# Score tiles begun by a ScalarE copy of the negated row maxima instead of a fourth product, with attention's steps in another order, in a one-core decoder layer

## The chip, the cores and the metric

One core of a Trainium2 chip runs the whole layer in one launch. The metric is device time in microseconds, the median of the runs of the program.

## What is computed

The reference is a decoder layer on `x` of 4 x 1024 x 256 (float32): attention with 16 heads of width 64, a convolution that shifts a memory, and a top-1 routed feed-forward layer, each followed by a layer norm. The change is in attention alone:

```python
q = einsum('bnd,hde->bhne', query, Wq) * scale
k = einsum('bmd,hde->bhme', query, Wk)
v = einsum('bmd,hde->bhme', query, Wv)
logits = einsum('bhne,bhme->bhnm', q, k)
attn = softmax(logits, axis=-1)
out = einsum('bhnm,bhme->bnhe', attn, v)
```

## The kernel before

**Units and halves.** Attention runs over 64 units. A unit is one pair of heads and 512 of the 1024 query tokens (`BANK`); its keys come in 8 tiles of 128. A unit is worked in two halves of four key tiles, so there are 128 halves, h = 0 to 127. All engines walk the same list of steps, `all_steps()`, each picking the steps that have work for it. Each half has its order written out by hand, in one of the four lines of `STEPS` (h modulo 4); a round below is four lines, two units.

**The steps** (functions of `build_attention`):
- `bite`: a projection of q, k or v, TensorE (lines 1123 and 1116) into a spare bank. q and k are kept as a high and a low float32r part. ScalarE copies the high part out (`bite_hi`, L1259), VectorE then makes the low part from the bank (`bite_lo`, L1315) and so frees the bank. For v ScalarE alone reads the bank.
- `pass`: 128 query rows against 512 keys with the high parts only, one matmul for each of the two heads (L1139), into two spare banks. It serves the row maxima of the unit ahead: VectorE reads each bank with a reduction by maximum (L1328), which frees it. After a unit's eighth pass VectorE negates and transposes the maxima (L1333, L1338), and SyncE moves them into `shift_rows` with four small DMAs (`move_shift`, L913).
- `score`: one tile of 128 keys x 512 queries x 2 heads into one of two score tiles `score_ps` (L1161). It takes four products, each a pair of matmuls with 64 rows, one for each head: k_hi q_hi, k_hi q_lo, k_lo q_hi, and ones times `shift_rows`, which adds the negated maximum of each query. ScalarE then takes the exponential of the tile (L1272).
- `av`: probabilities times v, full float32 (L1177). GpSimd sums the probabilities over the key tiles (`add`, L1033 and L1037, seven adds for a unit); `sum` adds them over partitions with a matmul of ones (L1188) into a spare bank.
- `sum`, `recip` and `norm` on VectorE: `turn_sum` transposes that bank into `sums` (L1357), `invert` takes the reciprocal (L1361) and transposes it back over `sums` (L1363), `normalise` multiplies `av_ps` by it into `o_out` (L1371), which SyncE stores.
- `early` and `late` are places into which the route's steps of the batch before are put: projection (L441, with a low part o_lo made by VectorE at L513), layer norms, the router's arithmetic.

**The three spare banks.** Every pass, bite of the steady part, `sum` and route product takes the next one or two of three banks in turn (`SPARE`, `take`). TensorE waits, ahead of the step's first matmul, until the last reader of each of them is through. A pass that takes banks 2 and 0 after a pass in 0 and 1 so waits for the reduction of the earlier pass's first head:

```python
def take(step, reads):
    for bank, (sem, value) in zip(SPARE[step], reads):
        if bank in last_read:
            pe.wait_ge(*last_read[bank])
        last_read[bank] = sem, value
```

The engines run their queues in order, so a wait holds back everything behind it.

Of the kernel before, what the change touches and what calls it, by code (L numbers as in the profile page):

```python
# [4 lines left out]
F32 = mybir.dt.float32  # L5
F32R = mybir.dt.float32r
# [4 lines left out]
P = 128  # L11
# [21 lines left out]
class Route:  # L33
# [639 lines left out]
def build_attention(nc, x, Wq, Wk, Wv, oT_dram, xT_dram, const, route, probs, v, weights, block, signals):  # L673
# [70 lines left out]
    def steps_of(h):  # L744
# [3 lines left out]
        for name in STEPS[h % 4]:  # L748
# [43 lines left out]
    with ExitStack() as ctx:  # L792
# [20 lines left out]
        o_out = sb("o_out", [P, 2, BANK])  # L813
# [3 lines left out]
        shift_rows = sb("shift_rows", [P, 2, BANK], F32R)  # L817
# [38 lines left out]
        max_found = sem("max_found")  # L856
        shift_in = [sem(f"shift_in{i}") for i in range(2)]
        score_ready = sem("score_ready")
# [30 lines left out]
        def _(sp):  # L889
# [16 lines left out]

            def move_shift(u):
                sp.wait_ge(max_done, u + 1)
                wait(sp, score_ready, KT * (u - 1))
                for r in range(P // BLOCK):  # L910
                    rows = neg_rows[r * BLOCK:r * BLOCK + 2 * JT, :]
                    heads = shift_rows[0:E + 1:E, u % 2, :].rearrange("h (j r i) -> h r j i", j=JT, i=BLOCK)
                    sp.dma_start(heads[:, r].bitcast(F32), rows.bitcast(F32)).then_inc(shift_in[u % 2], 16)  # L913

            def store_o(u):
                sp.wait_ge(o_done, u + 1)
                b, hp, c = u // (2 * PER_BATCH), u // 2 % PER_BATCH, u % 2
                sp.dma_start(oT_dram[b, hp, :, c * BANK:(c + 1) * BANK], o_out[:, u % 2, :]
# [32 lines left out]
            sp.wait_ge(rows_set, 2)  # L951
            move_shift(0)
            for h in range(HALVES):
# [24 lines left out]
                elif u + 1 < UNITS:  # L978
                    move_shift(u + 1)
                if h == 1:  # L980
# [23 lines left out]
        def _(pool):  # L1004
# [43 lines left out]
            pool.memset(o_out[:, :, :], 0.0).then_inc(rows_zeroed, 1)  # L1048
            pool.wait_ge(rows_zeroed, 2)
            pool.tensor_copy(one_rows[:, :], prob_sum[:, 0, 0, 0:P]).then_inc(rows_set, 1)  # L1050
            pool.tensor_copy(shift_rows[:, :, :], o_out[:, :, :]).then_inc(rows_set, 1)
# [31 lines left out]
        def _(pe):  # L1083
# [58 lines left out]
            def score(u, kt):  # L1142
# [5 lines left out]
                if kt == 0:  # L1148
                    pe.wait_ge(shift_in[u % 2], 64 * (u // 2 + 1))
# [947 lines left out]
```

## Time and profile before

| | |
|---|---|
| median of 3 runs (lowest, highest) | 1872.64 us (1872.44, 1873.9) |
| profiled execution, first to last instruction | 1867.0 us |
| around that span, to the median of the runs | 5.6 us |
| TensorE busy in the span | 98% |
| VectorE, ScalarE, GpSimd busy | 65%, 46%, 72% |
| mean granted TensorE clock, share of full | 0.996 |

The profiled execution has no whole time of its own beside its span; the runs outside the profile give that. Busy time of TensorE counts a matmul from its start to its modelled end, and neighbours overlap, so the distance between the starts of two matmuls, and not the duration of one, tells what each costs. In a timeline row the first number is the start, the second how long the row's instructions ran together, xN how many records it joins, and the bracket the idle time of the engine before it and what ended it. PEld is the weight load.

### The profile page before, as it was taken

The page shows a single profiled execution, that of the slowest core. Times are in us where ns is not written, and L with a number is a line of the kernel's source. Part 1 is how long each engine was busy: PE and PEld are TensorE (multiplying, and loading weights), DVE is VectorE, ACT ScalarE, POOL GpSimd, SP SyncE. Part 2 cuts the span into 40 slices and gives each one's busy share as a digit, 9 for nine tenths or more (in the row PEclk, how much of TensorE's full clock was granted, in tenths as well). Part 3 has the DMA queues.
Part 4 walks back from the last instruction along what each step waited for, and adds up shares of the span by engine and source line. Part 5 has one row for each costly group of instructions (what it writes and reads, how often), then busy time and mean ns, then how long its engine had stood idle before and what let it go on. Part 6 is the DMA issues. An engine that isn't in the chain of part 4 may idle for free.

```text
span 1867.0 us, 30732 instructions
## 1 busy us (share of the span) xinstructions
PE 1829.2 (98%) x11400; PEld 1163.7 (62%) x11400; DVE 1216.5 (65%) x2155; ACT 856.0 (46%) x1098; POOL 1339.4 (72%) x711
## 2 busy tenths in 40 slices
PE   7999999999999999999999999999999999999998
PEld 5555555555665555556666565556665555598887
DVE  6666666666666657766666657766666668765565
ACT  3444444444435443443345544443444534475775
POOL 2798778788767867788677767887668787652664
PEclk9999999999999999999999999999999999999999
DMA  4300000002211000022211000022111011453431
GB/s 118 128 24 18 24 18 24 18 24 85 91 46 46 24 18 24 21 81 87 70 45 42 18 7 24 24 80 65 50 39 42 18 35 35 125 159 106 161 136 35
DMA packets 132142, 104.24 MB, mean 56 GB/s; under 512 B 58140, under 2 KB 118684, under 8 KB 130972
## 3 DMA queue, kind: packets, MB, share of 16 engines
q1 hardware_dynamic: 128924, 93.81, 16.8%
q0 software_dynamic: 3072, 8.46, 1.3%
q8 instruction: 94, 1.54, 0.3%
q14 instruction: 52, 0.43, 0.1%
HBM read 69.15 MB, written 29.43 MB: 53 GB/s over the span
## 4 chain that ended last, share of the span: by engine, by line
PE 87%; DVE 4%; POOL 4%; issue 2%; ACT 2%; DMA 1%; SPq 0%; POOLq 0%; DVEq 0%; ACTq 0%
PE score_ps L1161 23%; PE av_ps L1177 23%; PE spare_ps L1123 9%; PE spare_ps L1139 8%; PE spare_ps L1116 4%; PE y_ps L1749 4%; PE spare_ps L441 4%; PE h_ps L1720 4%; PE spare_ps L1188 3%; POOL prob_sum L1037 3%; DVE max_of L1328 1%; PE spare_ps L490 1%; PE spare_ps L465 1%; PE score_ps L1123 0%; PE y_ps L441 0%
## 5 line engine op out<-in xcount | busy, mean ns | idle before, releaser
L1037 POOL TENSOR_TENSOR prob_sum<-prob_sum,probs 128x1024 f32<-128x1024 f32 (+1 forms) x384 | 907.3, 2363 | 196.7 <-ACT probs L1272 164.7
L1328 DVE TENSOR_REDUCE max_of<-spare_ps 128x1 f32<-128x512 f32 x1024 | 656.9, 683 | 336.1 <-PE spare_ps L1139 325.7
L1272 ACT ACTIVATE probs<-score_ps 128x1024 f32<-128x1024 f32 x512 | 502.6, 1026 | 664.4 <-PE score_ps L1161 653.0
L1177 PE MATMUL av_ps<-probs,v 128*64 128x512 f32 x2048 | 487.9, 602 | 2.2 <-ACT probs L1272 1.4
L1177 PEld LDWEIGHTS av_ps<-probs,v 128*64 128x64 f32 x2048 | 129.8, 136 | 240.3 <-issue 218.3
L1033 POOL TENSOR_TENSOR prob_sum<-probs 128x1024 f32<-128x1024 f32 (+1 forms) x64 | 150.4, 2350 | 144.2 <-ACT probs L1272 144.0
L1139 PE MATMUL spare_ps<-k_hi,q_hi 64*128 64x512 f32 x1024 | 227.9, 439 | 11.5 <-DVE max_of L1328 10.6
L1139 PEld LDWEIGHTS spare_ps<-k_hi,q_hi 64*128 64x128 f32 x1024 | 98.1, 184 | 213.1 <-issue 176.9
L1161 PE MATMUL score_ps<-q_hi,k_hi 64*128 64x512 f32 x1024 | 209.0, 403 | 0.2 <-ACT probs L1272 0.2
L1161 PE MATMUL score_ps<-shift_rows,ones 64*128 64x512 f32 x1024 | 203.5, 392 | 0.0
L1161 PE MATMUL score_ps<-q_lo,k_hi 64*128 64x512 f32 x1024 | 202.7, 391 | 0.0
L1161 PE MATMUL score_ps<-q_hi,k_lo 64*128 64x512 f32 x1024 | 202.7, 391 | 0.0
L1123 PE MATMUL spare_ps<-xT_kept,w_hi 128*128 128x512 f32 x496 | 155.9, 405 | 0.6
L1161 PEld LDWEIGHTS score_ps<-q_hi,k_hi 64*128 64x128 f32 x1024 | 97.0, 185 | 31.6 <-ACT probs L1272 15.8
L1161 PEld LDWEIGHTS score_ps<-shift_rows,ones 64*128 64x128 f32 x1024 | 97.0, 184 | 22.0
L1161 PEld LDWEIGHTS score_ps<-q_hi,k_lo 64*128 64x128 f32 x1024 | 96.8, 184 | 21.1
L1161 PEld LDWEIGHTS score_ps<-q_lo,k_hi 64*128 64x128 f32 x1024 | 96.8, 184 | 18.4
L1123 PEld LDWEIGHTS spare_ps<-xT_kept,w_hi 128*128 128x128 f32 x496 | 86.8, 189 | 32.3 <-issue 18.9
L1116 PE MATMUL spare_ps<-wv_hi,xT_kept 128*128 128x256 f32 x488 | 91.2, 289 | 1.3 <-issue 0.9
L1315 DVE SCALAR_TENSOR_TENSOR q_lo<-spare_ps,q_hi 128x512 fp32r<-128x512 f32 x62 | 42.9, 692 | 75.8 <-ACT q_hi L1259 75.6
L1116 PEld LDWEIGHTS spare_ps<-wv_hi,xT_kept 128*128 128x128 f32 x488 | 73.3, 191 | 13.8 <-issue 11.4
L1123 PE MATMUL spare_ps<-xT_kept,w_lo 128*128 128x512 f32 x248 | 77.8, 395 | 0.0
(278 smaller groups left out, 2367.7 us busy)
## 6 DMA issues: line engine op xcount, KB each, us to landing
o_transposed<-o_out SPq DMA_DIRECT2D x64, 256.0 KB, 2.0
v<-in_L_ffn_W_dram SPq DMA_DIRECT2D x16, 1024.0 KB, 5.6
o_in<-o_transposed SPq DMA_DIRECT2D x28, 512.0 KB, 4.1
w_raw<-in_L_attn_Wq_dram SPq DMA_DIRECT2D x64, 64.0 KB, 2.3
w_raw<-in_L_attn_Wk_dram SPq DMA_DIRECT2D x64, 64.0 KB, 2.2
wv_raw<-in_L_attn_Wv_dram SPq DMA_DIRECT2D x32, 128.0 KB, 3.0
shift_rows<-neg_rows SPq DMA_DIRECT2D x256, 1.0 KB
x<-in_x_dram SPq DMA_DIRECT2D x4, 1024.0 KB, 5.9
```

Source lines behind the costliest of these rows:

```text
L441: last = pe.matmul(bank[:, 0:self.D], a[:, c, :], w[:, c, :], start=(n == 0 and c == 0), stop=(n == 2 and c == self.CC - 1))
L1033: pool.tensor_tensor(out, probs[:, (n - 1) % RING, heads], probs[:, n % RING, heads], ALU.add).then_inc(prob_added, 1)
L1037: pool.tensor_tensor(out, out, probs[:, n % RING, heads], ALU.add).then_inc(prob_added, 1)
L1116: last = pe.matmul(bank[:, m * 4 * E:(m + 1) * 4 * E], xT[batch][:, half, kc, rows], w[:, kc, :], start=(i == 0 and kc == 0), stop=(i == 2 ...
L1123: last = pe.matmul(bank[:, :], w[:, of % 2, "qk".index(kind), kc, :], xT[batch][:, half, kc, cols], start=(i == 0 and kc == 0), stop=(i == ...
L1139: pe.matmul(bank[:, :], q_hi[rows, par, tokens], k_hi[rows, par, keys], start=True, stop=True).then_inc(pass_ready, 1)
L1161: last = pe.matmul(score_ps[n % 2][:, hd, :], a[rows], b[rows], start=(i == 0), stop=(i == len(products) - 1))
L1177: last = pe.matmul(av_ps[hd * E:(hd + 1) * E, :], v[:, quad % 2, kt, 2 * first_head + hd, :], probs[:, n % RING, hd, :], start=(kt == 0), ...
L1272: act.activation(probs[:, n % RING], score_ps[n % 2][:, :, :], ACT.Exp).then_inc(probs_ready, 1)
L1328: dve.tensor_reduce(max_of[:, u % 2, kh, j, hd:hd + 1], bank[:, :], AX.X, ALU.max).then_inc(pass_read, 1)
L1720: last = pe.matmul(h_bank(p, c)[:, rows], w[x][:, k, c * P:(c + 1) * P], xeT[y][:, k, rows], start=(i == 0 and k == 0), stop=(i == 2 and k ...
L1749: last = pe.matmul(y_place(p, t)[:, :], h[x][:, c, row:row + P], w[y][:, c, :], start=(c == 0 and i == 0), stop=(c == LAST and i == 2))
```

## The change

- `score` loses its fourth product from the third tile on. The first two tiles of all keep it, reading their shift from a piece of `route.o_hi`.
- A new step `seed` has ScalarE copy the shift, spread over all 128 partitions in `shift_all`, into the score tile two ahead; the three products then add to it. A seed waits for its tile's exponential, and a score for its seed.
- The maxima travel in two hops: four small DMAs into a scratch tensor `shifts` in HBM (`move_shift`), then one DMA of 512 KB that writes them to all partitions (`spread_shift`). SyncE waits between the two.
- `o_out` is gone: `normalise` writes over `sums`, and `turn_sum` waits for the store of the unit before.
- `STEPS` has a new order: scores always in pairs, each pair with a pass on both sides.

```diff
 STEPS = (
-    "early av av av pass score score pass sum av recip pass score score pass late bite bite",
-    "bite norm score pass early av pass score score pass score pass late av av av",
-    "av pass score score pass early av sum pass score score pass bite late av recip av",
-    "pass norm score score pass early bite bite av pass score score pass late av av av"))
+    "av pass score score seed seed pass early av av sum recip pass score score seed seed pass late av bite bite",
+    "norm pass score score seed seed pass early av av bite pass score score seed seed pass late av av",
+    "av pass score score seed seed pass early av av sum recip pass score score seed seed pass late av bite",
+    "norm pass score score seed seed pass early av av bite pass score score seed seed pass late av av bite"))
...
+            if name == "seed" and h < HALVES and KT * u + kt + 2 < KT * UNITS:
+                yield "seed", KT * u + kt + 2
...
             def move_shift(u):
                 sp.wait_ge(max_done, u + 1)
-                wait(sp, score_ready, KT * (u - 1))
+                wait(sp, shift_in[u % 2], 16 * (u // 2))
                 for r in range(P // BLOCK):
                     rows = neg_rows[r * BLOCK:r * BLOCK + 2 * JT, :]
-                    heads = shift_rows[0:E + 1:E, u % 2, :].rearrange("h (j r i) -> h r j i", j=JT, i=BLOCK)
-                    sp.dma_start(heads[:, r].bitcast(F32), rows.bitcast(F32)).then_inc(shift_in[u % 2], 16)
+                    heads = shift_dram[u % 2].rearrange("h (j r i) -> h r j i", j=JT, i=BLOCK)
+                    sp.dma_start(heads[:, r], rows.bitcast(F32)).then_inc(shift_out, 16)
+
+            def spread_shift(u):
+                sp.wait_ge(shift_out, 64 * (u + 1))
+                wait(sp, seeded, KT * (u - 1) - 2)
+                sp.dma_start(shift_all[:, u % 2], shift_dram[u % 2].rearrange("(a h) n -> a h n", a=1)
+                             .broadcast_to([P, 2, BANK])).then_inc(shift_in[u % 2], 16)
...
                 elif u + 1 < UNITS:
                     move_shift(u + 1)
+                    spread_shift(u + 1)
...
             def score(u, kt):
-                wait(pe, probs_ready, n - 1)
+                products = [(k_hi[:, par, keys], q_hi[:, par, tokens]), (k_hi[:, par, keys], q_lo[:, par, tokens]),
+                            (k_lo[:, par, keys], q_hi[:, par, tokens])]
                 if n < 2:
+                    pe.wait_ge(first_shift, 64)
...
+                    products.append((one_rows[:, :], shift_rows))
+                else:
+                    pe.wait_ge(seeded, n - 1)
...
+            def seed(n):
+
+                u, kt = divmod(n, KT)
+                if kt == 0 or n == 2:
+                    act.wait_ge(shift_in[u % 2], 16 * (u // 2 + 1))
+                act.wait_ge(probs_ready, n - 1)
+                act.activation(score_ps[n % 2][:, :, :], shift_all[:, u % 2], ACT.Copy).then_inc(seeded, 1)
...
             def turn_sum(u):
-                wait(dve, o_done, u)
+                wait(dve, o_stored[(u - 1) % 2], 16 * ((u + 1) // 2))
...
             def normalise(u):
-                dve.tensor_tensor(o_out[:, u % 2, :], av_ps[:, :], sums[:, :], ALU.mult).then_inc(o_done, 1)
+                dve.tensor_tensor(sums[:, :], av_ps[:, :], sums[:, :], ALU.mult).then_inc(o_done, 1)
```

The first place is TensorE from the tenth `sum` on (third line of `STEPS`): `spare_ps<-prob_sum,ones` is the sum, `spare_ps<-k_hi,q_hi` a pass, one row for each head. Before:

```order
L1177 MATMUL av_ps<-probs,v 64x512 x2
L1188 MATMUL spare_ps1<-prob_sum,ones 64x512 x2
L1139 MATMUL spare_ps2<-k_hi,q_hi 128x512
L1139 MATMUL spare_ps0<-k_hi,q_hi 128x512
...
L1161 MATMUL score_ps1<-shift_rows,ones 128x512 x2
L1139 MATMUL spare_ps1<-k_hi,q_hi 128x512
L1139 MATMUL spare_ps2<-k_hi,q_hi 128x512
```

And with the change:

```order
L1200 MATMUL av_ps<-probs,v 64x512 x4
L1211 MATMUL spare_ps0<-prob_sum,ones 64x512 x2
L1160 MATMUL spare_ps1<-k_hi,q_hi 128x512
L1160 MATMUL spare_ps2<-k_hi,q_hi 128x512
...
L1184 MATMUL score_ps1<-q_hi,k_lo 128x512 x2
L1160 MATMUL spare_ps0<-k_hi,q_hi 128x512
L1160 MATMUL spare_ps1<-k_hi,q_hi 128x512
```

Both have the sum, a pass, two score tiles and a pass; the two tiles now have six products in place of eight, and the last pass takes the sum's bank and the first bank of the pass before it, as it did.

The second place is VectorE at the same sum: `sums<-spare_ps` is `turn_sum`, the reciprocal and `sums<-inverse` are `invert`, `max_of<-spare_ps` reads one bank of a pass. Before:

```order
L1357 STREAM_TRANSPOSE sums<-spare_ps1 128x512
L1328 TENSOR_REDUCE max_of<-spare_ps2 128x1
L1328 TENSOR_REDUCE max_of<-spare_ps0 128x1
L1328 TENSOR_REDUCE max_of<-spare_ps1 128x1
L1328 TENSOR_REDUCE max_of<-spare_ps2 128x1
L1333 TENSOR_REDUCE neg_max<-max_of 128x8
L1338 STREAM_TRANSPOSE neg_rows<-neg_max 128x32
L1315 SCALAR_TENSOR_TENSOR q_lo<-spare_ps0,q_hi 128x512
L1361 RECIPROCAL inverse<-sums 128x16
L1363 STREAM_TRANSPOSE sums<-inverse 128x512
```

And with the change, up to the first pass of the next line:

```order
L1391 STREAM_TRANSPOSE sums<-spare_ps0 128x512
L1395 RECIPROCAL inverse<-sums 128x16
L1397 STREAM_TRANSPOSE sums<-inverse 128x512
L1361 TENSOR_REDUCE max_of<-spare_ps1 128x1
L1361 TENSOR_REDUCE max_of<-spare_ps2 128x1
...
L1348 SCALAR_TENSOR_TENSOR k_lo<-spare_ps2,k_hi 128x512
L1348 SCALAR_TENSOR_TENSOR k_lo<-spare_ps0,k_hi 128x512
L1404 TENSOR_TENSOR sums<-av_ps,sums 128x512
L1361 TENSOR_REDUCE max_of<-spare_ps1 128x1
L1361 TENSOR_REDUCE max_of<-spare_ps2 128x1
```

The inversion now stands between `turn_sum` and the reads of the pass behind the sum, and `normalise` directly between the low parts of the bites and the reads of the next line's first pass.

## Rows read from the trace of the kernel before

**Rows 1.** The page: the engines' busy line, the chain by engine.

```profile
PE 1829.2 (98%) x11400; PEld 1163.7 (62%) x11400; DVE 1216.5 (65%) x2155; ACT 856.0 (46%) x1098; POOL 1339.4 (72%) x711
...
PE 87%; DVE 4%; POOL 4%; issue 2%; ACT 2%; DMA 1%; SPq 0%; POOLq 0%; DVEq 0%; ACTq 0%
```

**Rows 2.** Busy time by window, one round: length, PE, PEld, DVE, ACT, POOL, clock, DMA.

```profile
320.98:366.81 45.83, 45.83 (x282) 26.25 (x280) 28.31 (x48) 19.28 (x23) 35.18 (x16) 1.00 0.06 18
```

**Rows 3.** Waits: us in all, times, longest.

```profile
PE spare_ps L1139 <- DVE max_of L1328: 10.6, 15, 1.6
```

**Rows 4.** Timeline from 388.90 us: sum, pass, two score tiles, pass, bite.

```profile
388.90 1.03 PE L1188 MATMUL spare_ps<-prob_sum,ones 128*64 128x512 f32 x4
...
389.86 0.50 PE L1139 MATMUL spare_ps<-k_hi,q_hi 64*128 64x512 f32 x2
389.98 0.72 DVE L1357 STREAM_TRANSPOSE sums<-spare_ps 128x512 f32<-128x512 f32 x1 [0.52 <-PE spare_ps L1188]
390.20 0.40 PE L1161 MATMUL score_ps<-q_hi,k_hi 64*128 64x512 f32 x2
...
391.35 1.94 ACT L1272 ACTIVATE probs<-score_ps 128x1024 f32<-128x1024 f32 x2 [2.45 <-PE score_ps L1161]
...
392.06 0.40 PE L1139 MATMUL spare_ps<-k_hi,q_hi 64*128 64x512 f32 x2
392.38 0.73 PE L1123 MATMUL spare_ps<-xT_kept,w_hi 128*128 128x512 f32 x2
```

**Rows 5.** Timeline from 393.97 us: what follows that bite of q.

```profile
393.97 1.94 PE L1177 MATMUL av_ps<-probs,v 128*64 128x512 f32 x8
394.08 0.60 ACT L1259 ACTIVATE q_hi<-spare_ps 128x512 fp32r<-128x512 f32 x1 [0.79 <-PE spare_ps L1123]
...
394.33 2.12 SPq L913 DMA_DIRECT2D shift_rows<-neg_rows  x4
394.71 0.69 DVE L1315 SCALAR_TENSOR_TENSOR q_lo<-spare_ps,q_hi 128x512 fp32r<-128x512 f32 x1 [0.41 <-ACT q_hi L1259]
```

**Rows 6.** Timeline from 368.19 us, VectorE: sum turned, inverted, the next pass read.

```profile
368.19 0.71 DVE L1357 STREAM_TRANSPOSE sums<-spare_ps 128x512 f32<-128x512 f32 x1
...
368.93 0.25 DVE L1361 RECIPROCAL inverse<-sums 128x16 f32<-128x16 f32 x1
...
369.86 1.25 DVE L1328 TENSOR_REDUCE max_of<-spare_ps 128x1 f32<-128x512 f32 x2
```

**Rows 7.** Timeline from 371.21 us: two bites of k, the second's low part, normalise.

```profile
371.21 0.72 PE L1123 MATMUL spare_ps<-xT_kept,w_hi 128*128 128x512 f32 x2
...
374.90 0.69 DVE L1315 SCALAR_TENSOR_TENSOR k_lo<-spare_ps,k_hi 128x512 fp32r<-128x512 f32 x1 [0.69 <-ACT k_hi L1259]
...
375.51 0.68 DVE L1371 TENSOR_TENSOR o_out<-av_ps,sums 128x512 f32<-128x512 f32 x1
```

**Rows 8.** Timeline from 666.73 us: three av, then a full-width matmul.

```profile
666.73 2.79 PE L1177 MATMUL av_ps<-probs,v 128*64 128x512 f32 x12
669.46 0.66 PE L479 MATMUL spare_ps<-ident,x 128*128 128x128 f32 x4
```

**Rows 9.** Timeline from 851.51 us: a pass held by VectorE.

```profile
851.51 1.25 DVE L1328 TENSOR_REDUCE max_of<-spare_ps 128x1 f32<-128x512 f32 x2
852.31 0.50 PE L1139 MATMUL spare_ps<-k_hi,q_hi 64*128 64x512 f32 x2 [1.61 <-DVE max_of L1328]
```

**Rows 10.** Busy time by window, columns as in rows 2, from that pass on.

```profile
852.00:860.00 8.00, 7.64 (x38) 5.54 (x40) 4.25 (x8) 1.32 (x3) 7.68 (x5) 0.79 0.33 109
```

**Rows 11.** Groups of instructions by shape: a ScalarE copy of 128x1024.

```profile
L332 ACT ACTIVATE o_hi<-o_in 128x1024 fp32r<-128x1024 f32 x24 | 25.5, 1061 | 49.4 <-PE spare_ps L441 49.4
```

**Rows 12.** Timeline at 378.08 us: four adds of GpSimd in a row.

```profile
378.08 10.00 POOL L1037 TENSOR_TENSOR prob_sum<-prob_sum,probs 128x1024 f32<-128x1024 f32 x4
```

**Rows 13.** DMA issues: KB each, median us to landing.

```profile
o_in<-o_transposed SPq DMA_DIRECT2D x28, 512.0 KB, 4.1
...
bp_all<-in_L_attn_bp_dram SPq DMA_DIRECT2D x1, 128.0 KB, 7.0
```

More of the change, by code:

```diff
@@ L670, in bites_of, with build_attention @@
     return [(kind, of, n) for kind, of, n in planned if of < (pairs // 2 if kind == "v" else pairs)]
-def build_attention(nc, x, Wq, Wk, Wv, oT_dram, xT_dram, const, route, probs, v, weights, block, signals):
+def build_attention(nc, x, Wq, Wk, Wv, oT_dram, xT_dram, shift_dram, const, route, probs, v, weights, block, signals):
     B, N, D = x.shape
@@ L816, in build_attention @@
         neg_rows = sb("neg_rows", [P, BLOCK], F32R)
-        shift_rows = sb("shift_rows", [P, 2, BANK], F32R)
+        shift_all = sb("shift_all", [P, 2, 2, BANK])
+        shift_rows = route.o_hi[:, :, :].rearrange("p c n -> p (c n)")[:, 0:BANK]
         score_ps = [ctx.enter_context(nc.psum_tensor(f"score_ps{i}", [P, 2, BANK], F32)) for i in range(2)]
@@ L856, in build_attention @@
         max_found = sem("max_found")
+        first_shift = sem("first_shift")
+        shift_out = sem("shift_out")
         shift_in = [sem(f"shift_in{i}") for i in range(2)]
+        seeded = sem("seeded")
         score_ready = sem("score_ready")
@@ L905, in load_wv, with move_first_shift @@
                                  ).then_inc(wv_loaded, 16)
+            def move_first_shift():
+                sp.wait_ge(max_done, 1)
+                for r in range(P // BLOCK):
+                    rows = neg_rows[r * BLOCK:r * BLOCK + 2 * JT, :]
+                    heads = shift_rows[0:E + 1:E, :].rearrange("h (j r i) -> h r j i", j=JT, i=BLOCK)
+                    sp.dma_start(heads[:, r].bitcast(F32), rows.bitcast(F32)).then_inc(first_shift, 16)
             def move_shift(u):
                 sp.wait_ge(max_done, u + 1)
-                wait(sp, score_ready, KT * (u - 1))
+                wait(sp, shift_in[u % 2], 16 * (u // 2))
                 for r in range(P // BLOCK):
                     rows = neg_rows[r * BLOCK:r * BLOCK + 2 * JT, :]
-                    heads = shift_rows[0:E + 1:E, u % 2, :].rearrange("h (j r i) -> h r j i", j=JT, i=BLOCK)
-                    sp.dma_start(heads[:, r].bitcast(F32), rows.bitcast(F32)).then_inc(shift_in[u % 2], 16)
+                    heads = shift_dram[u % 2].rearrange("h (j r i) -> h r j i", j=JT, i=BLOCK)
[5 more added lines that the diff above has]
+                             .broadcast_to([P, 2, BANK])).then_inc(shift_in[u % 2], 16)
             def store_o(u):
@@ L917, in store_o @@
                 b, hp, c = u // (2 * PER_BATCH), u // 2 % PER_BATCH, u % 2
-                sp.dma_start(oT_dram[b, hp, :, c * BANK:(c + 1) * BANK], o_out[:, u % 2, :]
+                sp.dma_start(oT_dram[b, hp, :, c * BANK:(c + 1) * BANK], sums[:, :]
                              ).then_inc(o_stored[u % 2], 16)
@@ L1160, in score @@
                         rows = slice(hd * E, (hd + 1) * E)
-                        last = pe.matmul(score_ps[n % 2][:, hd, :], a[rows], b[rows],
-                                         start=(i == 0), stop=(i == len(products) - 1))
+                        last = pe.matmul(score_ps[n % 2][:, hd, :], a[rows], b[rows], start=(n < 2 and i == 0),
+                                         stop=(i == len(products) - 1), skip_group_check=n > 1)
                 last.then_inc(score_ready, 1)
@@ L1286, in _ @@
                     exp(*at)
+                if name == "seed":
+                    seed(*at)
                 if name == "wp":
@@ L1336, in read_pass @@
                     dve.wait_ge(max_found, u + 1)
-                    wait(dve, shift_in[(u - 1) % 2], 64 * ((u + 1) // 2))
+                    wait(dve, first_shift, 64 if u > 0 else 0)
+                    wait(dve, shift_out, 64 * u)
                     dve.transpose(neg_rows[:, :].bitcast(F32), neg_max[:, :].bitcast(F32)).then_inc(max_done, 1)
@@ L2070, in build @@
         block = ctx.enter_context(nc.Block(no_gpsimd_drain=True))
-        build_attention(nc, x, Wq, Wk, Wv, oT_dram, xT_dram, const, route, probs, v, weights, block, signals)
+        build_attention(nc, x, Wq, Wk, Wv, oT_dram, xT_dram, shift_dram, const, route, probs, v, weights, block, signals)
         build_tail(nc, route, weights, probs, xe_dram, out, block)
```

12 lines of the change are left out of this document (5 added, 7 removed).

## The prediction

> **What bounds the kernel now.** I read the page first: TensorE is busy 98% of the span and carries 87% of the chain that ended last [rows 1]. Busy time of overlapping matmuls doesn't say that nothing waits, so I then took windows. The starts of the sums mark rounds of two units; in the stretch without route work a round lasts 45.83 us, TensorE is busy for all of it at full clock, VectorE for 28.3, ScalarE for 19.3 and GpSimd for 35.2 us [rows 2], and the next round is the same to 0.01 us. The reader is to see that TensorE is the bound here, and that VectorE has time to spare only as a sum. In the list of waits a pass was held by VectorE 15 times, for 10.6 us in all [rows 3]: its reads come in time, but the timeline shows how closely.
>
> **Products removed.** A score tile takes 2 x 4 products from 390.20 to 392.06 for two tiles: 1.86 / 8 = 0.23 us for each pair of matmuls [rows 4]. The 0.39 us that a single matmul is listed with overlaps its neighbour and is not what comes free. 16 tiles a round give 16 x 0.23 = 3.7 us; over 510 tiles 117 us.
>
> **Order of TensorE's work.** The new lines change between av or sum, bites, and scores or passes 22 times a round, the old ones 18 times. After three av (six starts of 0.43 = 2.58 us) a full-width matmul came 2.73 us after their start, so such a change costs 0.15 us [rows 8]; four more are 0.6 us, and about 0.3 us of small halts ahead of the second line's single scores go away with them. TensorE's own path for a round: 45.83 - 3.7 + 0.3 = 42.4 us.
>
> **Waits that this uncovers: the pass behind the sum.** Call the pass right after the sum B and the one after the next two scores C. C takes the bank of B's first head, which VectorE must have read. Before, `invert` stood behind both. Now it stands in front: from the sum's start, 1.08 us to `turn_sum` (388.90 to 389.98) [rows 4]; 0.74 to the reciprocal, 0.93 more to the read of B, 0.63 for its first head [rows 6]; then 0.2 until TensorE moves (851.51 + 0.63 = 852.14, pass at 852.31) [rows 9]. Together 3.58 us. TensorE's path from the sum's start: 0.96 to B, 0.34 to the first product [rows 4], 6 x 0.23 = 1.38, so 2.68. It waits 0.9 us, in lines 1 and 3: 1.8 us a round.
>
> **The first pass of lines 2 and 4.** Call it D and the one after its scores E, which takes D's first bank. VectorE's order is low parts of the bites, `normalise`, reads of D. With one bite (line 3 to 4) the low part starts 2.33 us after the bite (392.38 to 394.71) [rows 4, 5]; `normalise` follows 0.61 us after a low part (374.90 to 375.51) [rows 7], the read I take as another 0.61, then 0.63 and 0.2: 4.38 us. TensorE needs 1.59 us for the bite (392.38 to 393.97) [rows 4, 5], 0.34 and 1.38: 3.31. It waits 1.07 us. With two bites (line 1 to 2) the second low part starts at 3.69 us (371.21 to 374.90) [rows 7], so 5.74 against 1.59 + 1.38 + 1.72 = 4.69: 1.05 us. Before, a bite of v, which VectorE doesn't read, or a pass stood between. 2.1 us a round.
>
> **A round then:** 42.4 + 1.8 + 2.1 = 46.3 us against 45.8, half a microsecond more. The 3.4 us net that leave TensorE's path come back as 3.9 us of waits.
>
> **ScalarE.** No row shows it write to PSUM. The nearest is its copy of 128x1024 between SBUF tiles, 1.06 us [rows 11]; the exponential takes 0.97 us a tile in a row of two, from 1.15 us after its first product [rows 4], 0.92 with one product less. With seeds of 1.03 us the second seed ends 0.92 + 1.94 + 2.06 = 4.9 us after a pair begins; the second score needs it 0.69 us after the next pair's start, so pairs can follow every 4.3 us. The shortest distance in the new order is 4.8 us. Bounds: 0.6 us (a copy of half the size at its own rate) costs nothing; twice the copy, 2.1 us, would make each of eight pairs 6.4 us. I take 1.03, at no cost: bites' high parts fit into the gaps. The Trainium skill ("ScalarE: Activation LUTs", "ACT is a hardware spline evaluator") has the engine faster into PSUM than into SBUF; no row here shows it.
>
> **The shift's two hops.** After C, 2.3 us until the maxima leave (392.06 to 394.33), 2.1 us for the first hop [rows 4, 5], then 512 KB: 4.1 us by the load of that size, 7.0 us being the nearest broadcast (128 KB, behind other loads) [rows 13]. The first seed of the next unit comes 12.7 us after C in line 3, 14.1 in line 1, so 8.3 us are there for the spread: no cost, up to 1.6 us a unit if it took 9.9. SyncE is held some 2 us longer per unit; behind it are the store of the output, needed by the next `turn_sum` some 10 us later, and loads for the half after. I cost these, the in-place `normalise` and the two first tiles at nothing.
>
> **GpSimd.** Adds take 2.5 us in a row [rows 12]. A unit's last add ends 0.92 + 0.97 + 5.0 = 6.9 us after its last pair begins, the sum comes at 8.3. Covered, except where the route adds 2.5 us of its own.
>
> **Route stretches.** At 852.31 the old kernel shows the mechanism itself: o_lo, the inversion and the read in a row, and a pass held 1.61 us [rows 9]. VectorE's path now decides four times a round, so its route work (o_lo 2.1 us, the router's arithmetic) has less room: an estimate of 2 to 3 us a batch from that wait, 8 us in all.
>
> **Sum.** 31 rounds x 0.5 = 15, the last round without passes -3, route +8: +20 us on a span of 1867.0, so 1887; with the 5.6 us around it 1893 us. The profiled span plus those 5.6 is the median of the runs, so the sum holds against either.
>
> **Rivals.** *The reads keep up (faster).* The place is C and E in every line. What decides is their 3.9 us a round against 3.4 saved; if VectorE were 0.12 us quicker at each of the four, it would be even, and with none of the waits 1872.6 - 31 x 3.4 - 3 = 1764 us, with half of them about 1825. For it: VectorE is 62% busy in a round [rows 2]. Against it: each link of the chains has a row. 17%, most of it near 1825.
> *Even.* The same waits a little shorter: within 0.2% (3.7 us, about what a measurement of this kernel can tell), 1869 to 1876. 9%.
> *The clock falls.* In the 8 us after the pass held 1.61 us the granted clock is 0.79 in the mean [rows 10]; between the levels 2.4 and 1.2 GHz that is (1 - 0.79) x 8 / 0.5 = 3.4 us at the lower, a loss of 1.7 us. The new rounds have four shorter waits. Once a round it would cost 31 x 1.7 = 53 us: 1946. Against it: 15 such waits [rows 3] left a mean clock of 0.996. 13%.
> The Trainium skill ("TensorE: Matmul & The Clock Gate", "A second HAM failure mode: psum-queue depth-cycling") says that micro-idles between groups of matmuls can make the clock swing; by that rule it would be 1946 and not 1893, and at one place in this trace it agrees.
> *Seeds or spread bind (slower).* By the bounds above: 8 x 6.4 = 51.2 us a round, up to 2050 us; the late spread 64 x 1.6 = 100 us. 5%.
> My forecast has 56%.
>
> **How the numbers follow.** The forecast's own range is 1880 to 1912 (each of four waits 0.1 us off is 12 us, route work 0 to 15). To leave out no more than 2 in 10 the range reaches to 1862 and, towards the clock's case, to 1935. Faster by over 0.2% is the first rival, 0.17; within, 0.09; slower the rest, 0.56 + 0.13 + 0.05 = 0.74.
>
> **What would show it.** Right: rounds of about 46.3 us without route work; passes waiting for `max_of` some 120 times, about 0.9 and 1.1 us each, 120 us in all in place of 10.6; seeds near 1.03 us; TensorE busy about 92% of a round; the clock full. Wrong: rounds near 42.4 us and few such waits (the first rival); stretches at half clock; scores waiting for seeds; seeds waiting for `shift_all`; sums waiting for adds.

## The result, and the profile after

The changed kernel takes 1910.4 us (median of 4 runs, 1907.44 to 1912.03) against 1873.27 us for the kernel before beside it (1872.44 to 1875.66): 1.0205 times as long, interval 1.0193 to 1.0217. The change costs 37 us. The profiled execution spans 1909.2 us against 1867.0, which is 42 us; 4 of them are scatter. In the runs beside the experiments, where span and time of each are listed, the kernel before takes 1.7 to 2.9 us around its span and not 5.6, so the one that was profiled first was about 4 us shorter than usual.

The page of the changed kernel: busy time of the engines, and the chain by engine (answers to [rows 1]).

```profile
PE 1767.9 (93%) x10380; PEld 1074.6 (56%) x10380; DVE 1205.2 (63%) x2155; ACT 1323.6 (69%) x1608; POOL 1336.0 (70%) x711
...
PE 75%; DVE 11%; ACT 7%; issue 6%; DMA 1%; POOL 0%; SPq 0%; DVEq 0%; ACTq 0%
```

The same page's groups: max reads, exponentials, seeds (busy us and mean ns of one behind the bar).

```profile
L1361 DVE TENSOR_REDUCE max_of<-spare_ps 128x1 f32<-128x512 f32 x1024 | 656.7, 683 | 253.3 <-PE spare_ps L1160 236.2
L1295 ACT ACTIVATE probs<-score_ps 128x1024 f32<-128x1024 f32 x512 | 496.7, 1022 | 247.5 <-PE score_ps L1184 247.1
L1303 ACT ACTIVATE score_ps<-shift_all 128x1024 f32<-128x1024 f32 x510 | 504.3, 1034 | 1.0 <-DMA shift_all<-shifts 1.0
```

Busy time by window, one round without route work (columns as in [rows 2]).

```profile
327.08:373.87 46.79, 43.75 (x250) 23.39 (x248) 28.30 (x48) 33.99 (x39) 35.19 (x17) 1.00 0.14 40
```

TensorE now has 1020 fewer matmuls and is busy 93% instead of 98%, yet the round went from 45.83 [rows 2] to 46.79 us. VectorE's busy time in it did not change (28.31, 28.30), ScalarE's rose by 14.7 us, and the clock is full. The share of VectorE in the chain rose from 4% to 11%: the loss is in waits, and the list of waits says which.

Waits of the changed kernel: us in all, times, longest (the first answers to [rows 3]).

```profile
PE spare_ps L1160 <- DVE max_of L1361: 80.3, 113, 4.1
PE spare_ps L1160 <- ACT q_hi L1282: 23.2, 31, 1.1
...
PEld score_ps L1184 <- ACT score_ps L1303: 7.3, 9, 2.1
```

Timeline of the changed kernel from 350.28 us, TensorE and VectorE: the sum and the two passes behind it, and then one bite and passes D and E (score products left out).

```profile
350.28 1.03 PE L1211 MATMUL spare_ps<-prob_sum,ones 128*64 128x512 f32 x4
351.24 0.50 PE L1160 MATMUL spare_ps<-k_hi,q_hi 64*128 64x512 f32 x2
351.36 0.72 DVE L1391 STREAM_TRANSPOSE sums<-spare_ps 128x512 f32<-128x512 f32 x1 [1.38 <-PE spare_ps L1211]
352.11 0.25 DVE L1395 RECIPROCAL inverse<-sums 128x16 f32<-128x16 f32 x1
352.40 0.71 DVE L1397 STREAM_TRANSPOSE sums<-inverse 128x512 f32<-128x512 f32 x1
353.03 2.66 DVE L1361 TENSOR_REDUCE max_of<-spare_ps 128x1 f32<-128x512 f32 x4
353.83 0.50 PE L1160 MATMUL spare_ps<-k_hi,q_hi 64*128 64x512 f32 x2 [0.71 <-DVE max_of L1361]
354.26 1.08 PE L1200 MATMUL av_ps<-probs,v 128*64 128x512 f32 x4
355.27 0.72 PE L1144 MATMUL spare_ps<-xT_kept,w_hi 128*128 128x512 f32 x2
...
357.59 0.69 DVE L1348 SCALAR_TENSOR_TENSOR q_lo<-spare_ps,q_hi 128x512 fp32r<-128x512 f32 x1 [1.44 <-ACT q_hi L1282]
357.61 0.50 PE L1160 MATMUL spare_ps<-k_hi,q_hi 64*128 64x512 f32 x2 [0.69 <-ACT q_hi L1282]
358.20 0.68 DVE L1404 TENSOR_TENSOR sums<-av_ps,sums 128x512 f32<-128x512 f32 x1
358.80 2.69 DVE L1361 TENSOR_REDUCE max_of<-spare_ps 128x1 f32<-128x512 f32 x4
359.62 0.50 PE L1160 MATMUL spare_ps<-k_hi,q_hi 64*128 64x512 f32 x2
```

Read VectorE's rows down: between the sum it waited for (351.36) and the first read of pass B (353.03) stand the reciprocal and the transposition back. Pass C (353.83) cannot start before that read has freed its bank. The same with pass E (359.62): low part, `normalise`, then the reads of D. A wait can hide in such rows: E has no bracket here, yet starts 4.35 us after the bite (355.27), where TensorE's path is 3.31. Part of it is D's bracket, the rest lies before the record of the matmul.

**Where the 42 us between the two spans come from.** Eight route-free rounds at the start are 7.7 us longer (8 x 0.96). From the first sum to the last, before 68.07 to 1620.48, after 69.48 to 1658.47, the kernel gained 36.6 us in length; 31.5 rounds at 0.97 are 30.6, so 6 us are left to the route's stretches. Four of them are lost at one place near the end, where the router's arithmetic and a read stand ahead in VectorE's queue.

Timeline of the change from 1620.85 us: the read, and the pass that it holds.

```profile
1620.85 1.29 DVE L1361 TENSOR_REDUCE max_of<-spare_ps 128x1 f32<-128x512 f32 x2
1621.69 0.75 PE L1160 MATMUL spare_ps<-k_hi,q_hi 64*128 64x512 f32 x2 [4.10 <-DVE max_of L1361]
```

The first sum is 1.4 us later. The part behind the last sum, in which TensorE has the same 1588 matmuls, is 4.2 us longer (250.7 against 246.5), with a mean granted clock of 0.96 against 0.98 there: 4% of 250.7 is 10 us of clock lost, 2% of 246.5 is 5, so the clock accounts for these 4 us. That the change causes it is not shown.

### The profile page after: what moved, and what is told of

Read it like the earlier page. It is cut to its first block, busy times and chain, and to the rows that moved or that the text cites. A ratio compares the mean times of both kernels' runs of the same rounds, so it can differ in the third digit from the quotient of the medians.

```text
span 1909.2 us, 29394 instructions
## 1 busy us (share of the span) xinstructions
PE 1767.9 (93%) x10380; PEld 1074.6 (56%) x10380; DVE 1205.2 (63%) x2155; ACT 1323.6 (69%) x1608; POOL 1336.0 (70%) x711
## 4 chain that ended last, share of the span: by engine, by line
PE 75%; DVE 11%; ACT 7%; issue 6%; DMA 1%; POOL 0%; SPq 0%; DVEq 0%; ACTq 0%
PE av_ps L1200 22%; PE score_ps L1184 11%; PE spare_ps L1144 8%; PE spare_ps L1160 8%; PE spare_ps L1137 5%; PE y_ps L1782 5%; PE h_ps L1753 4%; PE spare_ps L441 4%; DVE max_of L1361 4%; PE spare_ps L1211 3%; DVE sums L1391 2%; ACT score_ps L1303 2%; ACT probs L1295 2%; DVE sums L1404 1%; ACT q_hi L1282 1%
## 5 line engine op out<-in xcount | busy, mean ns | idle before, releaser
L1295 ACT ACTIVATE probs<-score_ps 128x1024 f32<-128x1024 f32 x512 | 496.7, 1022 | 247.5 <-PE score_ps L1184 247.1
L1303 ACT ACTIVATE score_ps<-shift_all 128x1024 f32<-128x1024 f32 x510 | 504.3, 1034 | 1.0 <-DMA shift_all<-shifts 1.0
L1200 PE MATMUL av_ps<-probs,v 128*64 128x512 f32 x2048 | 503.7, 608 | 0.4 <-ACT probs L1295 0.4
L1160 PE MATMUL spare_ps<-k_hi,q_hi 64*128 64x512 f32 x1024 | 243.9, 468 | 116.9 <-DVE max_of L1361 80.3
L1200 PEld LDWEIGHTS av_ps<-probs,v 128*64 128x64 f32 x2048 | 122.1, 136 | 207.3 <-issue 154.2
L1391 DVE STREAM_TRANSPOSE sums<-spare_ps 128x512 f32<-128x512 f32 x64 | 45.9, 717 | 91.7 <-PE spare_ps L1211 91.7
L1277 ACT ACTIVATE v<-spare_ps 128x512 f32<-128x512 f32 x61 | 36.5, 599 | 74.7 <-PE spare_ps L1137 74.6
```

The lines of the kernel that those rows point to most:

```text
L1160: pe.matmul(bank[:, :], q_hi[rows, par, tokens], k_hi[rows, par, keys], start=True, stop=True).then_inc(pass_ready, 1)
L1200: last = pe.matmul(av_ps[hd * E:(hd + 1) * E, :], v[:, quad % 2, kt, 2 * first_head + hd, :], probs[:, n % RING, hd, :], start=(kt == 0), ...
L1295: act.activation(probs[:, n % RING], score_ps[n % 2][:, :, :], ACT.Exp).then_inc(probs_ready, 1)
L1303: act.activation(score_ps[n % 2][:, :, :], shift_all[:, u % 2], ACT.Copy).then_inc(seeded, 1)
L1391: dve.transpose(sums[:, :], bank[:, :]).then_inc(sum_turned, 1)
```

## The experiments

Twelve kernels ran, each beside the kernel before on the same chip. **V** is the theory of the prediction: VectorE's queue stands ahead of the reads that give a pass its bank. **S**: the seeds' load on ScalarE sets the round. **M**: more changes between kinds of matmul do. A round is the distance between the sums of one line in the stretch without route work.

| kernel | us | ratio to before (interval) | round |
|---|---|---|---|
| before | 1870.8 to 1873.3 | 1 | 45.83 |
| the change | 1910.4 | 1.0205 (1.0193 to 1.0217) | 46.79 |
| e1 recip behind | 1867.0 | 0.998 (0.9971 to 0.999) | 45.06 |
| e2 bites ahead of av | 1865.9 | 0.9973 (0.9963 to 0.9983) | 45.10 |
| e3 both | 1847.5 | 0.9868 (0.9849 to 0.9887) | 44.50 |
| e4 order alone | 1956.8 | 1.0451 (1.0434 to 1.0468) | 48.76 |
| e5 e3, half seeds | 1821.6 | 0.9726 (0.9709 to 0.9742) | 43.20 |
| e6 e3, seed behind bites | 1825.0 | 0.9755 (0.9732 to 0.9778) | 43.22 |
| e7 the change, half seeds | 1906.6 | 1.0184 (1.0167 to 1.0201) | 46.80 |
| e8 products alone | 1913.5 | 1.023 (1.0202 to 1.0258) | 47.26 |
| e9 e6, norm behind | 1831.8 | 0.9781 (0.9759 to 0.9804) | 43.7 |
| e10 norm behind | 1914.1 | 1.0217 (1.0193 to 1.024) | 47.1 |
| e11 e1, norm behind | 1871.8 | 0.9992 (0.998 to 1.0005) | 45.3 |
| e12 e8, half seeds | 1843.2 | 0.9844 (0.9827 to 0.986) | 44.28 |

**e1: recip back behind the second pass (lines 1 and 3).**

```diff
- ... av av sum recip pass score score seed seed pass late av bite bite
+ ... av av sum pass score score seed seed pass recip late av bite bite
```

> Edit: in lines 1 and 3 of the new order the inversion (recip) stands behind the second pair's pass instead of directly behind the sum; nothing else. Theory V (VectorE's queue in front of the pass that takes a bank back): sum to pass C falls from 3.55 us to TensorE's own 2.7, and the 0.11 us by which a held pass starts badly goes too, so a round is 46.8 - 2 x 1.0 = 44.8 us and the program 1910 - 31 x 2.0 = about 1848 us. Theory S (the seeds load ScalarE, whose loop of exponentials and seeds paces the pairs): the inversion isn't on its path, 1905 to 1912 us, and the wait moves to the scores. Theory M (more changes between kinds of matmul cost TensorE's own path): 1905 to 1912 us as well.

Measured 1867.0 us, 43 less where V had 62. C now starts 2.69 us behind the sum, TensorE's own time. The round lost 1.73 us and not the 2.0 expected: the two waits and the delay behind them are gone, but ScalarE's copy now comes later for D (0.90 us of wait after 0.69), and that takes 0.2 back.

Timeline of e1 from 345.75 us: pass D.

```profile
345.75 0.50 PE L1160 MATMUL spare_ps<-k_hi,q_hi 64*128 64x512 f32 x2 [0.90 <-ACT q_hi L1282]
```

S and M, by which nothing should move, fall as explanations of these two waits.

**e2: bites ahead of the last av.**

```diff
- ... pass late av bite bite        (line 3: ... late av bite)
+ ... pass late bite bite av        (line 3: ... late bite av)
```

> Edit: in lines 1 and 3 of the new order the last av stands behind the bites instead of ahead of them. Theory V: from the first bite to pass E VectorE's chain stays 5.7 us (two bites) and 4.35 us (one), but the 1.0 us of av now lies inside it, so a round loses 2 x 1.0 and twice the 0.11 us of a held pass: 44.6 us, program about 1842 us. Theory S: the pairs are then closer to each other and the scores wait for seeds instead, 1900 to 1912 us. Theory M: four changes of kind as before, 1905 to 1912 us.

Measured 1865.9 us, 44 less where V had 68; the round lost 1.69 of the 2.2 us expected.

**e3: both.**

> Both edits of the two runs beside it. Theory V: all four waits of a round go, TensorE's own path of 42.5 us is left, program 1910 - 31 x 4.2 = about 1780 us, less than the kernel before. Theory S: at pairs every 5.3 us ScalarE (34 of 42.5 us busy) begins to hold scores, 1820 to 1900 us. Theory M: 1905 to 1912 us.

Measured 1847.5 us: below both kernels, but 63 us less than the change where V had 130. The round lost 2.3 us and not the expected 4.2. Something had taken over. The time lies in the range that S had (1820 to 1900), but what waits is not what S says: scores waited 7.8 us for seeds, against these waits of passes.

Waits of e3 on TensorE.

```profile
PE spare_ps L1160 <- DVE max_of L1361: 26.6, 25, 4.1
...
PE spare_ps L1160 <- ACT q_hi L1282: 24.4, 22, 1.8
...
PE spare_ps L1160 <- DVE k_lo L1348: 14.8, 24, 1.5
```

Timeline of e3 from 341.44 us, ScalarE and TensorE: seeds, the bite of q and its copy, and the pass D that wants a bank.

```profile
341.44 1.97 ACT L1303 ACTIVATE score_ps<-shift_all 128x1024 f32<-128x1024 f32 x2
342.04 1.08 PE L1200 MATMUL av_ps<-probs,v 128*64 128x512 f32 x4
343.33 0.60 ACT L1282 ACTIVATE q_hi<-spare_ps 128x512 fp32r<-128x512 f32 x1
343.98 0.50 PE L1160 MATMUL spare_ps<-k_hi,q_hi 64*128 64x512 f32 x2 [0.86 <-ACT q_hi L1282]
```

The bite is done when the av starts (342.04), but ScalarE first finishes two seeds, and its copy (343.33 to 343.93) is what D waits for. By itself D would start 1.01 us behind the av, as elsewhere in this trace; it comes 1.94 behind. So the seeds do cost something once VectorE is out of the way: theory **V'**. Three kernels test it.

**e5: e3 with half seeds.** Each seed copies the rows of the first head only, so the second head's scores add to what the bank held (in e7 and e12 too).

```diff
- act.activation(score_ps[n % 2][:, :, :], shift_all[:, u % 2], ACT.Copy)
+ act.activation(score_ps[n % 2][:, 0, :], shift_all[:, u % 2, 0], ACT.Copy)
```

> e3 with each seed copying the first head's rows only (128x512 instead of 128x1024; the second head's scores then add to what the bank held, so the probabilities of that head are not the reference's). Theory V': in e3 VectorE holds nothing any more in the stretch looked at (sums 315.74 and 360.24), and what is left of the expected gain went to a new holder: ScalarE reads a bite's bank only behind two seeds (341.44 1.98, then q_hi 343.33), and the first pass of lines 2 and 4 waits for it (0.86 <- ACT q_hi, 0.32 <- DVE k_lo), with 0.3 and 0.1 more at the pass after. Seeds half as long end the bite's copy about 1 us sooner: 1.7 us per round x 32 = 54 off 1847.5, so about 1795 us. Rival M (what is left in e3 is the price of more changes between kinds of matmul, which no copy touches): 1847 as e3. Rival V (VectorE's queue still holds): 1840 to 1847.

Measured 1821.6 us, 26 less than e3, the round 1.30 less. The direction is V''s, the size half: the round kept 0.4 us more than expected, and 15 us of the 41 that 32 rounds would give did not come through in the stretches with route work.

**e6: the second seed behind the bites.** All work is done.

```diff
- ... score score seed seed pass recip late bite bite av   (line 3: bite av)
+ ... score score seed pass recip late bite bite seed av   (line 3: bite seed av)
```

> e3 with the second seed of the last score pair of lines 1 and 3 moved behind the bites, so that ScalarE reads a bite before it and not behind it; nothing left out. V': the hold of 0.86 after one bite goes wholly (q_hi starts at about 342.4 instead of 343.33), that of 0.32 after two bites partly, and the seed ends some 0.7 us later, before the second score product of the next pair needs it: 1.2 to 1.6 us per round x 32 = 38 to 51 off 1847.5, about 1800 us. If ScalarE's total time is what binds (rival S), moving a seed moves the wait to the scores: 1847, with waits of the scores for seeds in the trace.

Measured 1825.0 us, 22 less than e3 where 38 to 51 were expected: the round lost 1.28 us, as forecast, but only part of it came through in the stretches with route work. The round is that of e5 (43.22 and 43.20). It is not ScalarE's load but its order that e3 lost by: the same seeds, one of them two steps later, give what half the seeds' time gives. This is the best complete version: 2.4% faster than before, 4.5% faster than the change.

The window of one round of e6, and its chain by engine.

```profile
331.11:374.33 43.22, 43.03 (x251) 23.06 (x249) 27.84 (x48) 33.80 (x39) 35.23 (x17) 1.00 0.16 44
```

```profile
PE 67%; POOL 11%; DVE 7%; ACT 7%; issue 5%; DMA 2%; SPq 1%; POOLq 0%; DVEq 0%; ACTq 0%
```

TensorE is busy 43.03 of 43.22 us again, and GpSimd, 0% of the chain after the change, has 11% here. That the adds are the next bound, mostly in the route's stretches, is read from the trace; no run tested it. It begins before them: between 113 and 158 us, where GpSimd makes low parts of weights between its adds, the sum at 157.85 waits 1.30 us for the last add, and a round there takes 44.7 us.

**e7: the change with half seeds.**

> The changed kernel with each seed copying the first head's rows only (the second head's probabilities are not the reference's); 255 seeds lose about 0.5 us of ScalarE each, 130 us of its 1324. V: the passes wait for VectorE's queue, which no seed stands in; the 0.69 wait for q_hi in line 4 goes, but the pass behind it is held by VectorE to the same time: 1905 to 1910 us. S (the seeds' load on ScalarE set the 46.8 us round): 16 seeds x 0.5 = 8 us per round less at most, 2 us at least: 1700 to 1850 us.

Measured 1906.6 us, round 46.80. ScalarE's busy time fell from 1323.6 to 1108.3 us (510 seeds of 0.42 us less each; the count of 255 in my expectation was wrong) and the round stayed to 0.01 us.

Waits of e7 on TensorE, beside which those of the change stand above.

```profile
PE spare_ps L1160 <- DVE max_of L1361: 80.2, 112, 4.1
...
PE spare_ps L1160 <- ACT q_hi L1282: 21.3, 31, 0.7
```

The waits for VectorE are the same (80.2 and 80.3 us). D's wait for ScalarE, which I expected to go, stayed (21.3 us, 23.2 in the change): it runs from the bite through its copy, and no seed stands in it. In the change as made, S is false; the same 0.42 us a seed counts in e3 and not here, since here VectorE comes last.

**e4: the new order alone.** The kernel before with the new order and without its seeds: four products, the shift by the old DMAs.

> The kernel before with the new order of steps and no seeds: four products a tile, shift_rows and o_out as before. Theory V: of eight pairs a round four run in front of a pass that VectorE's chain holds anyway, so the fourth product costs 0.46 us only at the other four: a round is 46.8 + 1.84 = 48.6 us, program about 1967 us, and the products are worth half of 117 us in this order. Theory S: without seeds ScalarE has nothing to hold, the order costs nothing and the program is near the kernel before, 1873 to 1895 us. Theory M: 0.3 to 0.7 us a round on the kernel before, 1883 to 1895 us.

Measured 1956.8 us. The order alone costs 84 us, though it takes no work in.

Window of one round of e4, and its sum and pass C (the timeline).

```profile
337.42:386.18 48.76, 47.26 (x283) 26.61 (x280) 28.31 (x48) 19.19 (x22) 35.05 (x17) 1.00 0.06 17
```

```profile
361.58 1.03 PE L1188 MATMUL spare_ps<-prob_sum,ones 128*64 128x512 f32 x4
...
365.13 0.49 PE L1139 MATMUL spare_ps<-k_hi,q_hi 64*128 64x512 f32 x2 [0.25 <-DVE max_of L1328]
```

This pair of rows is the clearest proof of V. From the sum to C it is 365.13 - 361.58 = 3.55 us with four products a tile, and 353.83 - 350.28 = 3.55 us with three. Two pairs of matmuls of 0.23 us were taken out between them and the pass came not a hundredth sooner: VectorE sets its start.

**e8: the products alone.** The changed kernel in the order of before, seeds behind their scores.

```diff
+ "early av av av pass score score seed seed pass sum av recip pass score score seed seed pass late bite bite",
+ "bite norm score seed pass early av pass score score seed seed pass score seed pass late av av av",
+ "av pass score score seed seed pass early av sum pass score score seed seed pass bite late av recip av",
+ "pass norm score score seed seed pass early bite bite av pass score score seed seed pass late av av av"))
```

> The changed kernel's seeds and three products in the order of steps of the kernel before, a pair of seeds behind each pair of scores. The products take 3.7 us per round of 45.83 away, to 42.1. Against it, in this order two score steps come as little as one pass apart (line 2: score score pass score), while the bank of a score comes back only after an exp of 1.02 and a seed of 1.03 us, four operations for a pair: by the distances about 1 us held in each of lines 1 and 3, 2 to 3 us in line 2. Taken together 45 to 48 us per round, so 1850 to 1935 us, likeliest 1890. If the seeds fit anywhere (rival: ScalarE has room at 69% busy, so the order was not needed for them): 1873 - 118 = 1755 us.

Measured 1913.5 us, inside the range expected and 23 above its likeliest value. Its waits are of another kind.

Waits of e8: scores for their seeds.

```profile
PEld score_ps L1184 <- ACT score_ps L1303: 116.2, 118, 2.6
...
PE score_ps L1184 <- ACT score_ps L1303: 69.3, 39, 2.0
```

Timeline of e8 from 387.67 us, TensorE: the pass between two pairs of scores, the held score, and av.

```profile
387.67 0.39 PE L1160 MATMUL spare_ps<-k_hi,q_hi 64*128 64x512 f32 x2
390.01 0.50 PE L1184 MATMUL score_ps<-q_hi,k_hi 64*128 64x512 f32 x2 [1.95 <-ACT score_ps L1303]
...
391.15 4.06 PE L1200 MATMUL av_ps<-probs,v 128*64 128x512 f32 x10
```

Windows of e8: two halves of a round, and the 8 us around that hold.

```profile
352.11:374.96 22.85, 22.50 (x131) 11.65 (x127) 13.19 (x23) 15.96 (x19) 16.67 (x7) 1.00 0.16 46
374.96:399.37 24.41, 22.41 (x122) 11.72 (x122) 14.79 (x26) 18.14 (x21) 18.43 (x9) 0.93 0.11 34
```

```profile
388.00:396.00 8.00, 6.05 (x26) 2.14 (x24) 2.58 (x4) 4.95 (x6) 7.43 (x4) 0.79 0.01 4
```

In line 2 a single score comes one pass behind a pair (387.67, then 390.01). Its bank must be exponentiated and seeded first, and TensorE stands 1.95 us. Then the granted clock is at its lower level for a while (0.79 in the mean of 8 us): ten av matmuls take 4.06 us, 0.41 each, where [rows 8] have twelve in 2.79, 0.23 each. In the first eight rounds the half with this hold took 24.2 to 24.4 us five times and 22.7 three times, so the clock fell in five of eight. One fall costs 1.6 us, the difference of the two lengths. The mean clock of e8 is 0.975, against 0.994 in the change.

**e12: e8 with half seeds.**

> e8 with each seed copying the first head's rows only (the second head's probabilities are not the reference's). If e8's loss is the time that a score's bank takes to come back (exp 1.02, exp, seed 1.03, seed) and the clock that fell behind its holds of 1.94 us: the holds shorten by about 1 us each, the waits of scores for seeds (69.3 + 116.2 us in e8) fall to some 60 to 80 in all, and the mean clock goes from 0.975 back to about 0.99; 1913 less about 60 for the waits and 25 for the clock: about 1830 us. If the old order holds the passes by VectorE instead: 1900 to 1913.

Measured 1843.2 us, 70 less than e8 where 83 were expected; mean clock 0.990.

Waits of e12: scores for their seeds.

```profile
PEld score_ps L1184 <- ACT score_ps L1303: 73.8, 40, 2.1
...
PE score_ps L1184 <- ACT score_ps L1303: 54.9, 37, 1.6
```

The two lines count one hold twice, once for the weight load and once for its matmul: each of TensorE's own 37 waits has its weight load in the other line, as each of the 39 in e8. TensorE stood 54.9 us where e8 has 69.3. By either line the waits fell less than expected: only the first of a pair's two seeds stands in the held score's chain, so a hold shortens by what one seed loses and not two (1.61 us in this trace, after 1.95). The cause is settled all the same: in the old order the seed's duration, which e7 found to be worth 4 us in the new one, is worth 70. Nearly half of that is the clock: between the first sum and the last the granted clock was at its lower level, half the higher one, for 85.3 us in e8 and 20.5 in e12, which comes to 32 us.

**Norm behind the first pass of lines 2 and 4: e9 (on e6), e10 (on the change), e11 (on e1).**

```diff
- "norm pass score score seed seed pass early av av ...
+ "pass norm score score seed seed pass early av av ...
```

> e6 with norm put behind the first pass of lines 2 and 4 (VectorE reads that pass before it normalises); nothing left out. In e6 one hold of VectorE is left in a round looked at: 0.19, with 0.17 of following delay, at the pass behind the first one of the half after a single bite (338.83), where norm (0.67) stands ahead of the reads; after two bites it is 1.76 instead of 1.72. V: 0.4 to 0.5 us per round x 32 = 13 to 16 off 1825, about 1810 us. M: no change, 1825. If GpSimd's adds bind by now (11% of e6's chain, all of it stretches with routing), less comes through: 1815 to 1825.

> The changed kernel with norm behind the first pass of lines 2 and 4 and nothing else. V: what stands ahead of the reads that give the bank back to the second pass there is one or two bites, norm (0.68) and the reads; without norm the two holds of about 1.05 shrink to 0.4 each, 1.3 us per round less with the 0.1 that a hold costs the matmul behind it: 46.8 to 45.5, x 32 = 42 off 1910, about 1868 us; the two waits behind the sums stay. M or S: 1910.

> e1 (recip behind the second pass) with norm behind the first pass of lines 2 and 4 as well; the bites stay where the change put them. V: e1's round of 45.07 less 1.3 for norm: 43.8, 1867 - 1.3 x 32 = 1825 us, so that moving two VectorE steps behind reads is worth as much as e6's moves of bites and seeds. If the waits for ScalarE (q_hi, 0.9 in e1) take over as in e3: 1840.

All three missed: 1831.8, 1914.1 and 1871.8 us are 7, 4 and 5 us above their bases, where 15, 42 and 42 less were expected. The intervals of e10 and e11 overlap with those of their bases; that there is a loss at all is read from the rounds, which grew by 0.5, 0.3 and 0.3 us.

Timeline of e10 from 360.81 us: passes D and E and the av behind E, with VectorE's rows from its reads of D on.

```profile
360.81 0.50 PE L1160 MATMUL spare_ps<-k_hi,q_hi 64*128 64x512 f32 x2 [0.69 <-ACT q_hi L1282]
361.41 1.29 DVE L1361 TENSOR_REDUCE max_of<-spare_ps 128x1 f32<-128x512 f32 x2
362.52 0.41 PE L1160 MATMUL spare_ps<-k_hi,q_hi 64*128 64x512 f32 x2
362.62 0.68 DVE L1404 TENSOR_TENSOR sums<-av_ps,sums 128x512 f32<-128x512 f32 x1
363.40 1.94 PE L1200 MATMUL av_ps<-probs,v 128*64 128x512 f32 x8 [0.47 <-ACT probs L1295]
```

E is held no more: 362.52 - 360.81 = 1.71 us behind D, where the change has 359.62 - 357.61 = 2.01. But the av behind E starts a new unit in `av_ps`, which `normalise` must have read. It now ends at 363.30, and av starts at 363.40 instead of 0.32 behind E. The bracket names the exponentials, which were done long before; at the same place with two bites the trace names `sums`, 0.65 us. So `norm` has a due time on both sides, and the 1.3 us for it in my expectations was wrong: I had looked at who waits for the reads, and not at who waits for the step I moved.

## Why the prediction was right

**Right, and shown.** The sign and the mechanism. The four waits were there, by VectorE's chains: sum to C 3.55 us (predicted 3.58), one bite to E 4.35 (4.38), two bites to E 5.72 (5.74). e1 and e2 each took one pair away and each gave the round back 1.7 us; e4 shows the wait without any change in the products. There were 113 waits for `max_of` against some 120 predicted, and that the numbers are so near is partly luck: C and E make 96 of them, three places a round, since the E behind one bite has no bracket, and 17 waits elsewhere fill up the count. They are listed with 80 us instead of 120, since D's wait for ScalarE (23.2 us) and time without a bracket carry the rest. Seeds take 1.034 us (1.03 taken), the 512 KB spread lands in 4.0 us (4.1 taken), and nothing waited for it but 1.0 us in all. TensorE's 93% of a round was put at 92.

**Mis-sized.** On the spans the sum gave 1887 us and 1909.2 were measured. Of these 22 us, 16 are one term: "A round then ... half a microsecond more" was 0.97. After a pass that was held, av starts 0.43 us behind it (353.83 to 354.26), against 0.32 from a pass that was not to what follows (392.06 to 392.38 in [rows 4]). Four a round are 0.44 of the missing 0.5 us, some 14 us over 31 rounds.

Two more errors of a round cancel by luck. Added up from the pieces that nothing held, TensorE's own path is 42.7 us and not 42.4, in part because two bites take 3.17 us up to the pass behind them and not 2.97.

Timeline of the change from 332.07 us: two bites, D and E (score products left out).

```profile
332.07 0.73 PE L1144 MATMUL spare_ps<-xT_kept,w_hi 128*128 128x512 f32 x2
...
335.24 0.50 PE L1160 MATMUL spare_ps<-k_hi,q_hi 64*128 64x512 f32 x2
...
337.79 0.50 PE L1160 MATMUL spare_ps<-k_hi,q_hi 64*128 64x512 f32 x2 [0.67 <-DVE max_of L1361]
```

VectorE's chain being as forecast, a longer path means a shorter wait there: 0.87 us instead of 1.05. The four waits are 3.65 us together instead of 3.9.

The rest: "the last round without passes -3" did not show. The units without passes took 17.95 and 15.00 us where the kernel before has 18.05 and 15.18, since scores without passes between them wait for their seeds; all nine such waits in the list (7.3 us) stand there. The start and the part behind the last sum gave 6 us more, the route 6 us where 8 stood. The 5.6 us around the span are not a time of the kernel (1.7 us around the changed one's), and that hid 4 us of the error: by the medians 1893 is only 17 short.

**Not foreseen.** D in line 4 waits 0.69 us for ScalarE's copy of the bite just made. It costs nothing there, because VectorE holds E past it anyway, and the seeds are no part of it (e7). e3 shows its price once that cover is gone.

**The rivals.** *The reads keep up* fell with 113 waits, though its prices can be held against e3 and e6: taking all four waits away gave not 1764 but 1847, and 1825 with the seed moved as well. My 1764 counted waits as if nothing stood behind them. *The clock falls* did not happen in the change: the round shown has a clock of 1.00 in spite of its four waits. The Trainium skill ("TensorE: Matmul & The Clock Gate", "A second HAM failure mode: psum-queue depth-cycling") tells of a kernel whose clock swings because TensorE idles briefly and often between groups of matmuls. The trace of the change disagrees (mean clock 0.994), and e8 agrees behind its holds of 1.95 us. *Seeds bind* was given 5% for the new order, and e7 bears that out: 215 us less of ScalarE's work changed the time by 4 us, and the intervals overlap.

**What the two parts were worth.** In the old order going from four products to three costs 41 us (e8 against before), in the new one it saves 46 (the change against e4). The new order costs 84 us with four products; with three it makes no difference clear of noise (1910.4 against 1913.5 us, the intervals overlap). The seeds needed score pairs far apart, and the order that set them apart put `recip` and the bites where VectorE was late. With those moved (e6), order and products together are 47 us below the kernel before.

## What to carry to other kernels

Where banks rotate between engines that run in order, follow for every moved step both queues: what stands ahead of the read that frees the next bank, and who waits for the moved step itself. A wait that is removed uncovers the next one in line, so a gain from several removed waits is at most what the nearest following chain leaves, and only a run shows that chain. Work taken from the bounding engine between a release and the matmul that needs it (here 3.55 us with four products or three) saves nothing there.

## What was unexpected of the hardware

A held pass can cost more than its wait: 0.43 instead of 0.32 us until av starts behind it, at all four places of a round. It is not so for every held matmul: D, held 0.69 us, has its scores 0.34 us behind it (357.61 to 357.95), as a pass that nothing held. ScalarE's copy of 128x1024 into PSUM took 1.034 us against 1.061 between SBUF tiles [rows 11]. The Trainium skill ("ScalarE: Activation LUTs", "ACT is a hardware spline evaluator") has it faster into PSUM, and the trace agrees by 3%, though the two copies differ in the type they write as well. The clock fell behind holds of 1.94 and 1.95 us in e8 in five of eight rounds and stayed full behind holds of the same length in three. In e12 it stayed full behind eight of 1.60 and 1.61 us, while the kernel before shows a fall behind one of just that length [rows 9, 10]. The length of a hold alone thus doesn't tell whether the clock falls; what else does stays open here.
